# Windowed attention in a conv-attention-expert kernel: the mask product on 64 array rows, the products of a block grouped by array tile, the projection behind the second turn of the probabilities

## The chip, the cores and the metric

The kernel runs on one core of a Trainium2 chip. The time is device microseconds of one execution, given as the median of several. The profile shows one execution, with all engines of the core: TensorE (PE for its matrix products, PEld for its weight loads), VectorE (DVE), ScalarE (ACT), GpSimd (POOL) and the DMA queues.

## The reference, cut to what matters

Eight images of 64 channels and 32x32 pixels go through two deformable convolutions, then through windowed attention and then through a layer of experts. The change touches the attention alone:

```python
q  = (x @ Wq.T).reshape(b, t, h, e) / scale          # t = 1024 tokens, h = 8 heads, e = 64
kk = (xp @ Wk.T).reshape(b, tp, h, e) / scale        # xp: x padded by k-1 tokens ahead
v  = (xp @ Wv.T).reshape(b, tp, h, e)
idx = jnp.arange(t)[:, None] + jnp.arange(k)[None, :]     # k = 32: each token sees 32 keys
dot  = jnp.einsum('bthe,btkhe->bthk', q, kk[:, idx])
attn = jax.nn.softmax(dot, axis=-1)
out  = jnp.einsum('bthk,btkhe->bthe', attn, v[:, idx])
return out.reshape(b, t, h * e) @ Wu.T + bu
```

## The kernel before

The two convolutions come first (span 0 to about 415 us), then a layer norm, the attention (437 to 679 us), a second layer norm and the experts. Heads are folded into two sets of weights ahead of the attention: `a_heads` (queries times keys) and `b_heads` (values times the output projection).

The attention works on 32 blocks: 4 pairs of images, 8 blocks of 128 tokens each. Each block goes through a pipeline that is written out by hand, with one order per engine; a body of four blocks is looped seven times with a register, and an eighth body follows unrolled. Counting semaphores join the engines. On TensorE one block `b` of the loop (`body`, L908) does, in this order:

- `queries` of block b+4 (L821): eight products in fp32, each of 64 rows by 128 columns of the array, into banks 0 and 1 of the result memory. In the trace every fp32 product is two instructions, so a block shows 16.
- `values` of block b, image 0 (L888): eight products on array tiles of 64x64, into banks 5 and 6.
- `turn_probs` of block b+1, image 0 (L869): four transposes on the whole 128x128 array, into bank 4.
- `scores` of block b+3: two mask products in fp16 with 512 columns (L834), each on 32 rows by 128 columns, that start banks 2 and 3 with a large negative number where a key is outside a token's window; then sixteen products on 64x128 (L844) that add the scores.
- `values` of block b, image 1 (L888), then `turn_probs` of block b+1, image 1 (L869).
- `turn_keys` of block b+2 (L857): two transposes on 128x128 into bank 7.
- `project_values` of block b (L903): eight products on 128x64, into bank 7.

The waits of `values` stand in `before_values` (L873). In most blocks they are given as `carry`, so that they are written ahead of the last product of `queries` or of `scores`, and `values` itself starts with no wait.

ScalarE's block (L971) is: copies of the query results (L950), copy of the values of image 0 out of banks 5 and 6 (L968), copy of the turned probabilities of image 0 (L962), copy of the values of image 1, of the turned probabilities of image 1, and the exponentials of block b+3 (L956). VectorE's block (L1035) is: row maxima and their subtraction for block b+3 (L1007, L1009), copy of the turned keys (L1023), the join of the projection to the tokens (L1033), then sums and reciprocals for block b+3 (L1015, L1017). GpSimd scales the probabilities (L1085) and copies the windows of block b+4 onward (L1069, L1077).

Three lines set what `values` waits for. A copy of values raises `z_ready` by one (L968); VectorE raises it by one ahead of the loops (L1045); and `before_values` waits for a count (L878):

```python
    nc.vector.tensor_copy(at.mark[:, 0:1], m.bu[:, 0:1]).then_inc(at.z_ready, 1)      # L1045
                   m.ps[:, 5:7, image * 2 * P:(image + 1) * 2 * P]).then_inc(at.z_ready, 1)   # L969
        pe.wait_ge(at.z_ready, (i * BODY + b) * 2 + image + 1)                        # L878
```

Of the kernel before, what the change touches and what calls it, by code (L numbers as in the profile page):

```python
# [15 lines left out]
NIMG, C, H, W = 8, 64, 32, 32  # L16
PAIRS = NIMG // 2
P = 128
# [655 lines left out]
HG = 2  # L674
# [119 lines left out]

TURN_AHEAD, KEYS_AHEAD, SCORES_AHEAD, QUERIES_AHEAD = 1, 2, 3, 4
ALL_BLOCKS = PAIRS * BLOCKS
BODY = 4
TURNS = ALL_BLOCKS // BODY  # L800
# [4 lines left out]
def exists(i, b):  # L805

    return not isinstance(i, int) or i * BODY + b < ALL_BLOCKS


def attention_pe(nc, pe, m, at):  # L810
    def queries(i, b, carry=None):

        pe.wait_ge(at.windows_ready, i * BODY + b + 1)
        if b:
            pe.wait_ge(at.g_ready, (i * BODY + b) * 2)
        for h in range(H4):
            for image in range(2):
                rows = slice(C * image, C * image + C)
                if carry is not None and (h, image) == (H4 - 1, 1):
                    carry()  # L820
                last = nc.tensor.matmul(m.ps[:, image, h * P:(h + 1) * P], at.a_heads[rows, h, :],  # L821
                                        at.window[rows, b % 4, WINDOW:SPAN], start=True, stop=True)
                if h == H4 - 1:
                    last.then_inc(at.g_in_psum, 1)

    def scores(i, b, carry=None):

        pe.wait_ge(at.g_ready, (i * BODY + b) * 2 + 2)
        pe.wait_ge(at.swapped_ready, (i * BODY + b) * 2 + 2)
        if b:  # L830
            pe.wait_ge(at.shifted, i * BODY + b)
        for hg in range(HG):
            rows = slice(TQ * hg, TQ * hg + TQ)
            nc.tensor.matmul(m.ps[:, 2 + hg, :], m.spread_q[rows, :], m.mask[rows, :], start=True, stop=False,  # L834
                             skip_group_check=True)
        for image in range(2):
            for j in range(TILES):
                first = (image * TILES + j % 2 * 2 + j // 2) * KEYS
                for hg in range(HG):
                    rows = slice(C * hg, C * hg + C)  # L840
                    keys = at.window if image == hg else at.swapped
                    if carry is not None and (image, j, hg) == (1, TILES - 1, HG - 1):
                        carry()
                    last = nc.tensor.matmul(m.ps[:, 2 + hg, first:first + KEYS], at.g[rows, b % 2, image, j, :],  # L844
                                            keys[rows, b % 4, j * TQ:j * TQ + KEYS], start=False, stop=True,
                                            skip_group_check=True)
        last.then_inc(at.scores_in_psum, 1)

    def turn_keys(i, b):

        if b:
            pe.wait_ge(at.xw_ready, i * BODY + b)
        pe.wait_ge(at.windows_ready, i * BODY + b + 1)
        if b >= KEYS_AHEAD:
            pe.wait_ge(at.added, i * BODY + b)
        for odd in range(2):
            last = nc.tensor.transpose(m.ps[:, 7, (2 + odd) * P:(3 + odd) * P],  # L857
                                       at.window[:, b % 4, odd * TQ:odd * TQ + P], m.identity[:, :])
        last.then_inc(at.xw_in_psum, 1)

    def turn_probs(i, b, image):
        if image == 0:
            pe.wait_ge(at.probs_ready, i * BODY + b + 1)
        if b or image:
            pe.wait_ge(at.pt_ready, (i * BODY + b) * 2 + image)
        for odd in range(2):
            for hg in range(HG):
                k = odd * HG + hg
                last = nc.tensor.transpose(m.ps[:, 4, k * P:(k + 1) * P], at.p[:, b % SLOTS_P, hg, image, odd, :],  # L869
                                           m.identity[:, :])  # L870
        last.then_inc(at.pt_in_psum, 1)

    def before_values(i, b, image):  # L873

        pe.wait_ge(at.pt_ready, (i * BODY + b) * 2 + image + 1)
        if image == 0:
            pe.wait_ge(at.xw_ready, i * BODY + b + 1)
        pe.wait_ge(at.z_ready, (i * BODY + b) * 2 + image + 1)  # L878

    def values(b, image):  # L880

        for odd in range(2):
            first = (image * 2 + odd) * P
            for hg in range(HG):
                k = odd * HG + hg
                for late in range(2):
                    rows = slice(KEYS * late, KEYS * late + KEYS)
                    last = nc.tensor.matmul(m.ps[C * hg:C * hg + C, 5 + late, first:first + P],  # L888
                                            at.xw[rows, b % 2, odd, C * image:C * image + C],
                                            at.pt[rows, image, k * P:(k + 1) * P], start=True, stop=True,  # L890
                                            skip_group_check=True)
        last.then_inc(at.z_in_psum, 1)

    def project_values(i, b):
        pe.wait_ge(at.z_ready, (i * BODY + b) * 2 + 3)
        if not exists(i, b + KEYS_AHEAD):

            pe.wait_ge(at.added, i * BODY + b + 2)
            pe.wait_ge(at.xw_ready, ALL_BLOCKS)
        z = at.z[:, :, :].rearrange("p a (j h q) -> p a h j q", j=TILES, h=H4)  # L900
        for h in range(H4):
            for image in range(2):
                last = nc.tensor.matmul(m.ps[C * image:C * image + C, 7, 0:P],  # L903
                                        at.b_heads[:, h, :], z[:, image, h, :, :], start=(h == 0), stop=(h == H4 - 1),
                                        skip_group_check=True)
        last.then_inc(at.projected, 1)

    def body(i):  # L908
        for b in range(BODY):
            if exists(i, b + QUERIES_AHEAD):  # L910
                queries(i, b + QUERIES_AHEAD, lambda: before_values(i, b, 0))
            else:
                before_values(i, b, 0)
            values(b, 0)
            if exists(i, b + TURN_AHEAD):
                turn_probs(i, b + TURN_AHEAD, 0)
            if exists(i, b + SCORES_AHEAD):
                scores(i, b + SCORES_AHEAD, lambda: before_values(i, b, 1))
            else:
                before_values(i, b, 1)  # L920
            values(b, 1)
            if exists(i, b + TURN_AHEAD):
                turn_probs(i, b + TURN_AHEAD, 1)
            if exists(i, b + KEYS_AHEAD):
                turn_keys(i, b + KEYS_AHEAD)
            project_values(i, b)

    queries(0, 0)
    turn_keys(0, 0)
    queries(0, 1)  # L930
    scores(0, 0)
    turn_keys(0, 1)
    queries(0, 2)
    scores(0, 1)
    queries(0, 3)
    scores(0, 2)
    for image in range(2):
        turn_probs(0, 0, image)
    with pe.Fori(0, TURNS - 1) as i:
        body(i)  # L940
    body(TURNS - 1)


def attention_act(nc, act, m, at):
# [19 lines left out]
    def values(i, b, image):  # L964
        if image == 0:
            act.wait_ge(at.projected, i * BODY + b + 1)
        act.wait_ge(at.z_in_psum, (i * BODY + b) * 2 + image + 1)
        nc.scalar.copy(at.z[:, image, :].rearrange("p (a n) -> p a n", a=2),  # L968
                       m.ps[:, 5:7, image * 2 * P:(image + 1) * 2 * P]).then_inc(at.z_ready, 1)  # L969

    def body(i):  # L971
        for b in range(BODY):
            if exists(i, b + QUERIES_AHEAD):
                queries(i, b + QUERIES_AHEAD)
            values(i, b, 0)
            if exists(i, b + TURN_AHEAD):
                probs(i, b + TURN_AHEAD, 0)
            values(i, b, 1)
            if exists(i, b + TURN_AHEAD):
                probs(i, b + TURN_AHEAD, 1)  # L980
            if exists(i, b + SCORES_AHEAD):
                exponentials(i, b + SCORES_AHEAD)

    queries(0, 0)
    queries(0, 1)
# [1 line left out]
    exponentials(0, 0)  # L987
    queries(0, 3)
    exponentials(0, 1)
    exponentials(0, 2)  # L990
    for image in range(2):
        probs(0, 0, image)
    with act.Fori(0, TURNS - 1) as i:
# [292 lines left out]
def program(nc, a, out):  # L1286
    ctx = ExitStack()
    with ctx:
# [3 lines left out]
        def sem(name):  # L1292
            return ctx.enter_context(nc.semaphore(name))
# [173 lines left out]
        at.z_ready = sem("at_z_ready")  # L1467
        at.projected = sem("at_projected")
        at.added = sem("at_added")
        at.windows_ready = sem("at_windows_ready")  # L1470
        at.swapped_ready = sem("at_swapped_ready")
        at.exp_ready = sem("at_exp_ready")
# [308 lines left out]
def constants():  # L1781
# [17 lines left out]
    places = places.reshape(4, 2, TAPS, HALVES, HALF_PIX).swapaxes(2, 3).copy()  # L1799
    c["places"] = (places.reshape(4, 2, TAPS * PIX).view(np.uint32) >> 16).astype(np.uint16)  # L1800
    c["identity"] = np.eye(P, dtype=f32)
    c["spread_q"] = np.tile(np.eye(TQ) * MASK_SCALE, (P // TQ, P // TQ)).astype(f16)

    qq, kk = (np.arange(P) % TQ)[:, None], np.arange(KEYS)[None, :]
    c["mask"] = np.tile(np.where((kk > qq) & (kk <= qq + WINDOW), 0.0, MASKED), (1, TILES * HG)).astype(f16)
# [59 lines left out]
```

## Time and profile before

| | us |
|---|---|
| median of 3 runs | 744.38 (742.71 to 757.19) |
| the profiled execution | 749.22 |
| its span | 747.4 |
| mean granted TensorE clock in it | 0.870 of full speed |

Busy time is the sum over an engine's instructions where they don't overlap. Products on TensorE are pipelined and their ends are modelled, so the starts of groups are the safer reading: the time from one group's start to the next group's start is what a group takes of TensorE. In a row of the timeline the first number is the start and the second the length, both in us; "x16" is the number of instructions merged, and the bracket at the end gives the idle time of the engine before the row and what ended it.

### The profile page before, as it was taken

What the parts mean: (1) busy time and instruction counts of PE and PEld (TensorE: products, weight loads), DVE (VectorE), ACT (ScalarE), POOL (GpSimd) and SP (SyncE); (2) the same over time, 40 slices, a digit from 0 to 9 for tenths busy, and PEclk for the clock granted to TensorE, in tenths of its full rate; (3) what the DMA queues carried; (4) which work ended last, traced back from release to release, by engine and by line L of the source; (5) the groups of instructions that cost most, each with busy time, mean ns of one, the idle gap of its engine ahead of it and who ended that gap; (6) DMA issues with size and microseconds to landing.
All of it is one profiled execution on the core that took longest, in us unless ns stands there. A gap on an engine that the chain in (4) does not pass through costs nothing.

```text
span 747.4 us, 32556 instructions
## 1 busy us (share of the span) xinstructions
PE 637.9 (85%) x14954; PEld 474.3 (63%) x14954; DVE 462.7 (62%) x559; ACT 366.7 (49%) x564; POOL 293.1 (39%) x287
## 2 busy tenths in 40 slices
PE   6579888889895899899889487999999999995575
PEld 1146666667651577666668466888888888874353
DVE  0587877675615977777862715576666666665623
ACT  0265566454423655646642324565565565554430
POOL 4045556463510654554551232434434444430400
PEclk9856999896998588979988755999999999998768
DMA  8310000000004000000000720000000000000002
GB/s 300 81 29 3 5 4 5 4 4 4 5 4 89 10 4 4 4 4 5 5 4 4 163 94 1 3 1 0 0 0 0 0 0 0 0 1 1 1 2 117
DMA packets 6403, 18.01 MB, mean 24 GB/s; under 512 B 1869, under 2 KB 4237, under 8 KB 5573
## 3 DMA queue, kind: packets, MB, share of 16 engines
q1 hardware_dynamic: 6286, 16.24, 7.9%
q8 instruction: 99, 1.62, 0.9%
q14 instruction: 18, 0.15, 0.1%
HBM read 12.37 MB, written 3.87 MB: 22 GB/s over the span
## 4 chain that ended last, share of the span: by engine, by line
PE 77%; DVE 6%; ACT 5%; DMA 4%; issue 4%; POOL 1%; SPq 1%; DVEq 0%; ACTq 0%
PE banks L268 21%; PE banks L199 11%; PE banks L844 9%; PE banks L821 5%; PE banks L888 5%; PE banks L869 5%; PE banks L903 4%; PE banks L171 3%; PE banks L185 2%; DMA off<-in_places_dram 2%; ACT y L301 2%; PE banks L834 1%; DMA off<-offsets_dram 1%; PE banks L229 1%; PE banks L615 1%
## 5 line engine op out<-in xcount | busy, mean ns | idle before, releaser
L322 POOL TENSOR_TENSOR y<-hy,hx 128x576 f32<-128x576 f32 (+1 forms) x104 | 167.4, 1631 | 201.1 <-DVE hy L396 191.8
L268 PE MATMUL banks<-y,xt 32*64 32x144 f32 (+1 forms) x6656 | 168.9, 309 | 23.3 <-issue 12.0
L268 PEld LDWEIGHTS banks<-y,xt 32*64 32x64 f32 x6656 | 115.6, 147 | 54.3 <-issue 35.4
L322 DVE TENSOR_TENSOR y<-hy,hx 128x576 f32<-128x576 f32 (+1 forms) x104 | 121.8, 1215 | 5.0 <-DVE hy L396 0.5
L1085 POOL TENSOR_TENSOR y<-y,stats 128x1024 f32<-128x1024 f32 x32 | 60.8, 1900 | 109.2 <-DVE stats L1017 109.2
L349 ACT ACTIVATE hx<-banks 128x768 f32<-128x768 f32 x96 | 62.0, 650 | 60.7 <-PE banks L171 59.7
L354 ACT ACTIVATE hy<-banks 128x768 f32<-128x768 f32 (+1 forms) x92 | 71.7, 805 | 38.8 <-PE banks L185 38.4
L301 DVE COPY y<-banks 128x768 f32<-128x768 f32 x48 | 45.8, 954 | 70.7 <-PE banks L268 70.7
L199 PE MATMUL banks<-y,w_dc 64*64 64x128 f32 x2304 | 85.8, 302 | 3.3 <-issue 2.0
L199 PEld LDWEIGHTS banks<-y,w_dc 64*64 64x64 f32 x2304 | 76.1, 152 | 10.7 <-issue 8.7
L1007 DVE TENSOR_REDUCE stats<-banks 128x16 f32<-128x1024 f32 x32 | 39.2, 1225 | 69.4 <-PE banks L844 69.4
L844 PEld LDWEIGHTS banks<-src,y 64*128 64x128 f32 x1024 | 64.5, 201 | 7.9 <-issue 7.9
L844 PE MATMUL banks<-src,y 64*128 64x64 f32 x1024 | 69.1, 289 | 0.0
L968 ACT COPY hy<-banks 128x512 f32<-128x512 f32 x64 | 38.0, 593 | 62.5 <-PE banks L888 62.5
L396 DVE TENSOR_SCALAR hy<-hy 128x1632 f32<-128x1632 f32 (+2 forms) x48 | 45.7, 953 | 10.3 <-ACT hy L354 10.2
L956 ACT ACTIVATE y<-y 128x1024 f32<-128x1024 f32 x32 | 33.8, 1057 | 27.1 <-DVE y L1009 27.1
L1015 DVE TENSOR_REDUCE stats<-y 128x16 f32<-128x1024 f32 x32 | 38.9, 1217 | 12.9 <-ACT y L956 12.9
L869 PE MATMUL banks<-identity,y 128*128 128x128 f32 x256 | 42.9, 291 | 3.1 <-ACT hy L962 3.1
L301 ACT COPY y<-banks 128x768 f32<-128x768 f32 x48 | 38.1, 794 | 14.3 <-PE banks L268 14.3
L888 PE MATMUL banks<-hy 64*64 64x128 f32 x1024 | 42.7, 282 | 1.7 <-ACT hy L968 1.7
L393 DVE TENSOR_SCALAR hx<-hx 128x1152 f32<-128x1152 f32 x48 | 38.9, 810 | 8.2 <-ACT hx L349 8.2
L821 PE MATMUL banks<-src,s 64*128 64x128 f32 x512 | 41.7, 308 | 1.7 <-ACT src L745 1.1
(140 smaller groups left out, 811.4 us busy)
## 6 DMA issues: line engine op xcount, KB each, us to landing
src<-in_x_dram SPq DMA_DIRECT2D x4, 578.0 KB, 5.7
y<-in_w_dram SPq DMA_DIRECT2D x1, 2080.0 KB
xt<-in_xt_dram SPq DMA_DIRECT2D x1, 2048.0 KB, 11.2
off<-in_w_dram SPq DMA_DIRECT2D x2, 1024.0 KB
out_dram<-tokens SPq DMA_DIRECT2D x4, 512.0 KB, 3.8
offsets_dram<-tokens SPq DMA_DIRECT2D x32, 54.0 KB
off<-offsets_dram SPq DMA_DIRECT2D x16, 108.0 KB
w_dc<-in_w_dc_dram SPq DMA_DIRECT2D x2, 288.0 KB, 9.4
```

Source lines behind the costliest of these rows:

```text
L199: last = nc.tensor.matmul(m.ps[C * g:C * g + C, bank + p // 2, 0:PLACES], cv.w_dc[rows, tap, :], m.sampled[rows, row % 2, p, tap, :], star ...
L268: last = nc.tensor.matmul(ap(out, [[UNIT_ROWS * PITCH - 2, 3], [PITCH, strip.n], [1, WIN_COLS]]), m.xt[32 * j:32 * j + 32, strip.tile_row, ...
L301: return copy(ap(m.sampled[:, unit.row % 2, j, 3 * unit.ky, :], [[TAPS * PLACES, 2], [W, 3 * UNIT_ROWS], [1, W]]), ap(m.ps[:, j, 4:], [[BA ...
L322: multiply(dst, hy, hx, ALU.mult).then_inc(cv.s_ready[g], 1)
L349: nc.scalar.activation(m.hx[:, u % 2, :, first:end], m.ps[:, bank:bank + 2, 0:end - first], ACT.Abs).then_inc(cv.emptied, 1)
L354: nc.scalar.activation(ap(m.hy[:, u % 2, 0, strips[0].at * HAT_ROW:], [[Y_HATS, 2], [HAT_PITCH, 3 * n_rows], [1, W]]), ap(m.ps[:, bank, :] ...
L396: nc.vector.tensor_scalar(hat, hat, 1.0, 1.0, ALU.min, ALU.subtract).then_inc(cv.hats, 1)
L821: last = nc.tensor.matmul(m.ps[:, image, h * P:(h + 1) * P], at.a_heads[rows, h, :], at.window[rows, b % 4, WINDOW:SPAN], start=True, stop ...
L844: last = nc.tensor.matmul(m.ps[:, 2 + hg, first:first + KEYS], at.g[rows, b % 2, image, j, :], keys[rows, b % 4, j * TQ:j * TQ + KEYS], st ...
L869: last = nc.tensor.transpose(m.ps[:, 4, k * P:(k + 1) * P], at.p[:, b % SLOTS_P, hg, image, odd, :], m.identity[:, :])
L888: last = nc.tensor.matmul(m.ps[C * hg:C * hg + C, 5 + late, first:first + P], at.xw[rows, b % 2, odd, C * image:C * image + C], at.pt[rows ...
L1085: nc.gpsimd.tensor_tensor(p, p, scale.unsqueeze(2).to_broadcast([P, 2 * TILES * HG, KEYS]), ALU.mult).then_inc(at.probs_ready, 1)
```

## The change

Five things change, all in the attention.

- `spread_q` is laid out in blocks of 64 rows (32 of the scaled identity, 32 of zeros), and the two mask products use rows 0 to 63 and 64 to 127, as the score products do.
- TensorE's order in a block is: `values` of both images, `turn_probs` of image 0, `queries`, `scores`, `turn_probs` of image 1, `turn_keys`, `project_values`. The `carry` arguments are gone.
- `before_values` ends with a semaphore instruction, `sem_inc` on a new semaphore `values_begun` that nobody waits for, and stands directly ahead of each `values`.
- ScalarE's order in a block is: both copies of values, the exponentials, the turned probabilities of image 0, the query copies, the turned probabilities of image 1.
- The exponentials run for block b+2 instead of b+3 (`EXPS_AHEAD`), so the one of block 2 leaves the part ahead of the loop. VectorE's and GpSimd's code is as before.

```diff
-TURN_AHEAD, KEYS_AHEAD, SCORES_AHEAD, QUERIES_AHEAD = 1, 2, 3, 4
+TURN_AHEAD, KEYS_AHEAD, EXPS_AHEAD, SCORES_AHEAD, QUERIES_AHEAD = 1, 2, 2, 3, 4
...
         for hg in range(HG):
-            rows = slice(TQ * hg, TQ * hg + TQ)
+            rows = slice(C * hg, C * hg + C)
             nc.tensor.matmul(m.ps[:, 2 + hg, :], m.spread_q[rows, :], m.mask[rows, :], start=True, stop=False,
                              skip_group_check=True)
...
         pe.wait_ge(at.z_ready, (i * BODY + b) * 2 + image + 1)
+        pe.sem_inc(at.values_begun, 1)
...
         for b in range(BODY):
-            if exists(i, b + QUERIES_AHEAD):
-                queries(i, b + QUERIES_AHEAD, lambda: before_values(i, b, 0))
-            else:
-                before_values(i, b, 0)
-            values(b, 0)
+            for image in range(2):
+                before_values(i, b, image)
+                values(b, image)
             if exists(i, b + TURN_AHEAD):
                 turn_probs(i, b + TURN_AHEAD, 0)
+            if exists(i, b + QUERIES_AHEAD):
+                queries(i, b + QUERIES_AHEAD)
             if exists(i, b + SCORES_AHEAD):
-                scores(i, b + SCORES_AHEAD, lambda: before_values(i, b, 1))
-            else:
-                before_values(i, b, 1)
-            values(b, 1)
+                scores(i, b + SCORES_AHEAD)
...
         for b in range(BODY):
+            for image in range(2):
+                values(i, b, image)
+            if exists(i, b + EXPS_AHEAD):
+                exponentials(i, b + EXPS_AHEAD)
+            if exists(i, b + TURN_AHEAD):
+                probs(i, b + TURN_AHEAD, 0)
             if exists(i, b + QUERIES_AHEAD):
                 queries(i, b + QUERIES_AHEAD)
-            values(i, b, 0)
-            if exists(i, b + TURN_AHEAD):
-                probs(i, b + TURN_AHEAD, 0)
-            values(i, b, 1)
             if exists(i, b + TURN_AHEAD):
                 probs(i, b + TURN_AHEAD, 1)
-            if exists(i, b + SCORES_AHEAD):
-                exponentials(i, b + SCORES_AHEAD)
...
     exponentials(0, 1)
-    exponentials(0, 2)
...
-    c["spread_q"] = np.tile(np.eye(TQ) * MASK_SCALE, (P // TQ, P // TQ)).astype(f16)
+    spread = np.concatenate([np.eye(TQ) * MASK_SCALE, np.zeros((C - TQ, TQ))])
+    c["spread_q"] = np.tile(spread, (P // C, P // TQ)).astype(f16)
```

## Rows read from the trace of the kernel before

**Rows 1.** Page, part 4: the chain of work that ended last, by engine, then line.

```profile
PE 77%; DVE 6%; ACT 5%; DMA 4%; issue 4%; POOL 1%; SPq 1%; DVEq 0%; ACTq 0%
```

**Rows 2.** Busy time by stretch: stretch, length, five engines (instructions), granted clock, DMA.

```profile
443.00:460.00 17.00, 16.09 (x134) 14.12 (x132) 6.60 (x7) 6.17 (x9) 2.16 (x2) 0.50 0.00 1
480.00:640.00 160.00, 160.00 (x2491) 130.90 (x2487) 105.69 (x139) 96.35 (x162) 65.57 (x93) 1.00 0.00 0
660.00:680.00 20.00, 16.90 (x274) 12.86 (x272) 9.73 (x17) 10.73 (x18) 3.80 (x2) 1.00 0.01 2
```

**Rows 3.** Timeline of TensorE's products, one block of the loop and the next start.

```profile
487.56 1.16 PE L821 MATMUL banks<-src,s 64*128 64x128 f32 x16
488.65 0.67 PE L888 MATMUL banks<-hy 64*64 64x128 f32 x16
489.25 0.66 PE L869 MATMUL banks<-identity,y 128*128 128x128 f32 x4
489.84 0.39 PE L834 MATMUL banks<-mask,spread_q 32*128 32x512 f16 x2
490.15 2.00 PE L844 MATMUL banks<-src,y 64*128 64x64 f32 x32
492.08 0.67 PE L888 MATMUL banks<-hy 64*64 64x128 f32 x16
492.68 0.66 PE L869 MATMUL banks<-identity,y 128*128 128x128 f32 x4
493.17 0.38 PE L857 MATMUL banks<-identity,src 128*128 128x128 f32 x2
493.49 1.09 PE L903 MATMUL banks<-hy,y 128*64 128x128 f32 x16
494.51 0.38 PE L821 MATMUL banks<-src,s 64*128 64x128 f32 x2
```

**Rows 4.** Timeline of all engines, the last block (31).

```profile
675.47 0.67 PE L888 MATMUL banks<-hy 64*64 64x128 f32 x16
...
676.26 0.59 ACT L968 COPY hy<-banks 128x512 f32<-128x512 f32 x1 [1.25 <-PE banks L888]
676.96 0.46 PEld L888 LDWEIGHTS banks<-hy 64*64 64x64 f32 x16 [1.06 <-issue]
676.99 0.67 PE L888 MATMUL banks<-hy 64*64 64x128 f32 x16 [0.85 <-ACT hy L968]
677.71 0.58 ACT L968 COPY hy<-banks 128x512 f32<-128x512 f32 x1 [0.87 <-PE banks L888]
678.35 0.85 PEld L903 LDWEIGHTS banks<-hy,y 128*64 128x64 f32 x16 [0.94 <-ACT hy L968]
```

**Rows 5.** Timeline of the other engines, in and behind the block of rows 3.

```profile
487.77 1.06 ACT L956 ACTIVATE y<-y 128x1024 f32<-128x1024 f32 x1 [0.76 <-DVE y L1009]
...
488.86 1.22 DVE L1015 TENSOR_REDUCE stats<-y 128x16 f32<-128x1024 f32 x1 [0.43 <-ACT y L956]
...
490.51 1.90 POOL L1085 TENSOR_TENSOR y<-y,stats 128x1024 f32<-128x1024 f32 x1 [2.77 <-DVE stats L1017]
...
492.20 1.22 DVE L1007 TENSOR_REDUCE stats<-banks 128x16 f32<-128x1024 f32 x1 [1.84 <-PE banks L844]
```

**Rows 6.** Timeline of all engines, ahead of the loop and in its first block.

```profile
460.52 1.11 PE L869 MATMUL banks<-identity,y 128*128 128x128 f32 x4
...
463.15 1.06 ACT L956 ACTIVATE y<-y 128x1024 f32<-128x1024 f32 x1 [5.53 <-DVE y L1009]
464.12 0.57 ACT L962 COPY hy<-banks 128x512 f32<-128x512 f32 x1
...
464.68 1.90 POOL L1085 TENSOR_TENSOR y<-y,stats 128x1024 f32<-128x1024 f32 x1 [3.98 <-DVE stats L1017]
...
464.74 1.12 PE L869 MATMUL banks<-identity,y 128*128 128x128 f32 x4 [3.10 <-ACT hy L962]
...
474.74 0.67 PE L888 MATMUL banks<-hy 64*64 64x128 f32 x16
```

More of the change, by code:

```diff
@@ L810, in attention_pe, with queries @@
 def attention_pe(nc, pe, m, at):
-    def queries(i, b, carry=None):
+    def queries(i, b):
         pe.wait_ge(at.windows_ready, i * BODY + b + 1)
@@ L818, in queries @@
                 rows = slice(C * image, C * image + C)
-                if carry is not None and (h, image) == (H4 - 1, 1):
-                    carry()
                 last = nc.tensor.matmul(m.ps[:, image, h * P:(h + 1) * P], at.a_heads[rows, h, :],
@@ L824, in queries, with scores @@
                     last.then_inc(at.g_in_psum, 1)
-    def scores(i, b, carry=None):
+    def scores(i, b):
         pe.wait_ge(at.g_ready, (i * BODY + b) * 2 + 2)
@@ L841, in scores @@
                     keys = at.window if image == hg else at.swapped
-                    if carry is not None and (image, j, hg) == (1, TILES - 1, HG - 1):
-                        carry()
                     last = nc.tensor.matmul(m.ps[:, 2 + hg, first:first + KEYS], at.g[rows, b % 2, image, j, :],
@@ L1469, in program @@
         at.added = sem("at_added")
+        at.values_begun = sem("at_values_begun")
         at.windows_ready = sem("at_windows_ready")
```

## The prediction

> **What bounds the kernel now.** I read the page's chain of work first: TensorE stands on 77% of it [rows 1], so time is to be looked for there. Then the busy time by stretch: between 480 and 640 us TensorE is busy for 160.00 of 160.00 us at a granted clock of 1.00, the full 2.4 GHz, while VectorE has 105.69, ScalarE 96.35 and GpSimd 65.57 [rows 2]. So in the loop TensorE alone sets the time, and the other three are hidden as long as none of them makes it wait. Then the timeline of one block. From one `queries` to the next it takes 494.51 - 487.56 = 6.95 us, and the starts of the groups divide it [rows 3]: queries 1.09, values of image 0 0.60, turn 0.59, mask 0.31, scores 1.93, values of image 1 0.60, second turn with keys and projection 1.83 (492.68 to 494.51). All 27 full blocks look alike.
>
> The reader is to see one more thing there. The second turn is followed by the turned keys, which use the same 128x128 tile, and takes 0.49 us (492.68 to 493.17); the first turn is the same four products, is followed by the mask on another tile, and takes 0.59 [rows 3]. So a change of array tile costs about 0.10 us. A block before has eight of them.
>
> **The change part by part.** *Fewer changes of tile.* In the new order they are: values to turn, turn to queries, scores to turn, keys to projection, projection to values; five instead of eight. Two of the three that go are queries to mask and mask to scores, because the mask now has the scores' tile; the third lies between the two groups of values. Queries then take 1.09 - 0.10 = 0.99, the mask 0.31 - 0.10 = 0.21. The mask's count, columns and type stay, so nothing else in it changes. No row shows fp16 products between fp32 ones on one tile: if the change of type empties the array as the change of tile did, these 0.20 us stay. If entering a group costs as well, the gain is larger. I bound the gain by 0 and 0.30 per block for both, the upper end being three times the 0.10 of rows 3, and take 0.20, because the rows show a price for the tile and none for the type.
>
> *The values of both images in a row.* This is what decides. `before_values` for image 1 waits for `z_ready` of 2b + 2. One of these counts comes from the mark ahead of the loop, 2b from the copies of earlier blocks; the last one can only be this block's copy of image 0. So image 1 may not start before ScalarE has copied image 0 out of banks 5 and 6, and that copy waits for image 0's products. Before, `turn_probs` and `scores` stood between the two, 492.08 - 488.65 = 3.43 us of work [rows 3], and covered this round trip. The new order puts nothing between. What it costs uncovered, the trace shows once, in the last block, where nothing is left to put there [rows 4]: image 0 starts at 675.47, the copy runs from 676.26 for 0.59 us, the weights of image 1 follow at 676.96 and its products at 676.99. Start to start that is 1.52 us, with TensorE idle for 0.85 of it. I take 1.52 for every block; ScalarE is free for the copy, as shown below, so the same steps follow each other.
>
> The Trainium skill ("PSUM — Partial Sum Buffer", Terms) says that TensorE writing and ScalarE reading one bank and quadrant at the same time is an error; no run here shows such an overlap, and by this rule the wait can't simply be dropped.
>
> *The semaphore instruction.* No row shows one that raises a count on TensorE. The two per block sit where waits sit already. In rows 4 the way from the copy's end (676.85) to the weight load (676.96), with a wait passed on it, is 0.11 us and is in the 1.52. So the bounds are nothing and another 0.11 per block; I take nothing, as nobody waits for this semaphore and the products ahead are queued already.
>
> *The new block*, from values of image 0: image 1 at 1.52, first turn at 2.12 (+0.60), queries at 2.71 (+0.59), mask at 3.70 (+0.99), scores at 3.91 (+0.21), second turn at 5.84 (+1.93), next block at 7.67 (+1.83). That is 0.72 longer than 6.95.
>
> *Is something else late next?* ScalarE copies image 0 at 0.79 to 1.38 and image 1 (0.72 after its products, rows 4) at 2.24 to 2.83; the exponentials follow, 1.06 [rows 5], to 3.89; then the turned probabilities, 0.57 [rows 6], to 4.5, which the second turn needs at 5.84. The query copies wait behind these two and are needed one block later. The last copy of turned probabilities can't start before the second turn and is done by about 7.1; image 1 of the next block needs it at 9.19. The exponentials run a block later, and VectorE's sums wait in order for them, with the next row maxima queued behind: sums start at 3.95, and from them to GpSimd's start is 490.51 - 488.86 = 1.65 [rows 5], so VectorE is free at about 5.5; the scores of that block end and release the maxima at 3.91 + 2.05 = 5.96 (490.15 to 492.20, rows 3 and 5). Cover 0.5 us. GpSimd ends at 5.6 + 1.90 = 7.5, and the turn that needs it stands at 7.67 + 2.12. So the moved exponentials cost nothing in the loop. No DMA is moved, and GpSimd's queue keeps its order.
>
> *Ahead of the loop.* The second turn of block 0 waited until 464.74 for a copy that stood behind the exponentials of block 2 (463.15) [rows 6]; without them it runs straight behind the first turn of 460.52. But the first turn of block 1 needs GpSimd's product, done at 464.68 + 1.90 = 466.58, and queries and scores now stand behind it. At full clock the next values follow 0.59 + 0.99 + 0.21 + 1.93 + 1.83 = 5.55 later, at 472.2; if the clock stays at half, as it was granted up to 460 [rows 2], up to some 3 us later. I take 474.0 against 474.74: -0.7.
>
> *The end.* From 474.74 to the last projection at 678.35 are 203.61 us [rows 4, 6]. New: 27 blocks of 7.67 are 207.09. Block 28 has no queries: 7.67 - 0.99 = 6.68. Block 29 has no queries and no scores; its second turn waits for the copy behind the exponentials, 3.89 + 0.57 + 0.05 = 4.52, and the block ends 1.83 later, at 6.35. Block 30: image 1's copy to 2.83, turned probabilities to 3.42, second turn at 3.47, then 0.59 and 1.02 (493.49 to 494.51): 5.08. Block 31 is the one of rows 4: 2.88. The sum is 228.08, so +24.47; with -0.7 it is **+23.8 us**.
>
> The profiled execution took 749.22, which gives 773.0. It lies 4.8 above the median shown, and the attention is alike in all of them as far as one trace can tell, so I predict on the median: 744.38 + 23.8 = **768**.
>
> **The rivals.** *Not slower: the second values start on the heels of the first.* Then a block is 6.95 - 0.30 = 6.65 and the kernel gains 27 x 0.30 = 8 us, and about 1 at the ends: 735. It decides as soon as image 1 starts less than 0.80 after image 0 (1.52 - 0.72). For it: the price of a change of tile in rows 3 is plain. Against it: it needs image 0's copy to be no condition, and the count and rows 4 say it is one. The Trainium skill ("TensorEngine Tiling (Array Packing)", Key Properties) states that changing the tiling mode drains TensorE; the 0.59 against 0.49 agree, and by that rule alone the change could only gain.
>
> *The stall is partly covered*, for instance because the copy starts earlier in a dense block than in the last one. Each 0.3 us per block takes 27 x 0.3 = 8 off: 755 to 759.
>
> *Dearer groups*: the fp16 mask still empties the array (0.20 x 28 = 5.6), or the semaphore instruction is on the path (0.11 x 31 = 3.4): 772 to 777.
>
> *The clock falls.* TensorE has a hole of 0.85 us in each block where it had none, and before the loop it was busy for 16.09 of 17.00 us and still granted 0.50, half of 2.4 GHz [rows 2]. At half clock the products take nearly twice as long; if a fifth of the attention ran so, about 40 us of it, some 25 more: 793. Against it: from 660 to 680, with 3.1 us of holes in 20, the grant stayed 1.00 [rows 2].
>
> **How the numbers follow.** Forecast 0.65 (its own range 764 to 772); dearer groups 0.15; clock 0.05; stall partly covered 0.10; on the heels 0.05. The range leaves out the clock case, the second values on the heels and a little of the rest: 756 to 780. The runs before spread from 742.71 to 757.19, so about 2% (15 us) is what can be told from no change. Slower by over 2%, above 759.3: 0.65 + 0.15 + 0.05 = 0.85. Within 2%: the partly covered stall and some of the last case, 0.12. Faster by over 2%, below 729.5: 0.03, should its price of a tile be double.
>
> **What would show it.** In the loop's timeline: image 1 of the values 1.5 us behind image 0, its idle time put down to L968's copy; about 0.99 from queries to mask and 0.21 from mask to scores; a block of 7.67 at a clock of 1.00; TensorE idle for 0.85 us in each block, and VectorE's maxima still released by the scores. I am wrong if image 1 follows within 0.8 us, if TensorE waits for VectorE or GpSimd, or if the clock drops in the loop.

## The result and the profile after

The changed kernel takes 762.25 us (median of 4 runs, 757.20 to 765.58) against 748.39 for the kernel before on the same chips (4 runs, 742.71 to 757.19): a ratio of 1.019 with a 95% interval from 1.013 to 1.026, so it is slower by 10 to 19 us. The range of the prediction holds it. Its centre, 768, was 6 us too high, and its +23.8 us was 10 too much; that only 6 of these 10 show is luck, since the median before, 744.38 when the forecast was made, is 748.39 with a fourth run. The result lies below the 764 to 772 of the forecast's own case. The prediction gave 0.85 to slower by over 2% and 0.12 to within 2%; the measured 1.9% stands at the bound between the two, with an interval on both sides of it. The profiled execution took 760.81 us, with a span of 758.9.

The chain of work, from the page of the changed kernel, now has 7% in which TensorE waited for nothing that the profile shows ("issue"), where it had 4% [rows 1]:

```profile
PE 74%; issue 7%; DVE 6%; ACT 5%; DMA 4%; POOL 2%; SPq 1%; DVEq 0%; POOLq 0%
```

Busy time by stretch in the changed kernel (columns as in rows 2): three stretches ahead of the loop, then the loop.

```profile
441.00:448.50 7.50, 6.87 (x56) 6.19 (x57) 0.42 (x1) 2.15 (x4) 1.12 (x4) 0.50 0.01 4
449.00:458.00 9.00, 6.08 (x96) 5.49 (x96) 6.48 (x7) 5.55 (x7) 0.00 (x0) 1.00 0.01 2
459.00:468.00 9.00, 6.46 (x54) 4.59 (x54) 4.12 (x5) 3.63 (x6) 4.86 (x8) 0.50 0.00 0
480.00:640.00 160.00, 142.53 (x2308) 121.32 (x2304) 96.43 (x129) 88.08 (x148) 59.84 (x88) 1.00 0.00 0
```

In the loop TensorE is busy for 142.53 of 160 us where it had no hole at all [rows 2], still at a granted clock of 1.00. The timeline of one block, all engines, shows where the hole is (the line numbers are the changed kernel's: L885 values, L962 their copy, L865 turns, L819 queries, L832 mask, L840 scores, L853 keys, L900 projection):

```profile
502.85 0.67 PE L885 MATMUL banks<-hy 64*64 64x128 f32 x16
...
503.64 0.59 ACT L962 COPY hy<-banks 128x512 f32<-128x512 f32 x1 [1.34 <-PE banks L885]
...
504.30 0.45 PEld L885 LDWEIGHTS banks<-hy 64*64 64x64 f32 x16 [1.02 <-issue]
504.33 0.67 PE L885 MATMUL banks<-hy 64*64 64x128 f32 x16 [0.81 <-issue]
...
504.93 0.65 PE L865 MATMUL banks<-identity,y 128*128 128x128 f32 x4
...
505.51 1.16 PE L819 MATMUL banks<-src,s 64*128 64x128 f32 x16
...
506.50 0.38 PE L832 MATMUL banks<-mask,spread_q 64*128 64x512 f16 x2
506.51 1.97 PEld L840 LDWEIGHTS banks<-src,y 64*128 64x128 f32 x32
...
506.72 1.90 PE L840 MATMUL banks<-src,y 64*128 64x64 f32 x32
...
508.55 0.66 PE L865 MATMUL banks<-identity,y 128*128 128x128 f32 x4
508.67 1.23 DVE L1000 TENSOR_REDUCE stats<-banks 128x16 f32<-128x1024 f32 x1 [0.53 <-PE banks L840]
...
509.35 1.09 PE L900 MATMUL banks<-hy,y 128*64 128x128 f32 x16
...
510.38 0.67 PE L885 MATMUL banks<-hy 64*64 64x128 f32 x16
```

Image 1 of the values starts 504.33 - 502.85 = 1.48 us behind image 0. The copy of image 0 lies between them, from 503.64 to 504.23. It is the pattern of rows 4, now in every block. The profile calls the gap "issue". The likely reason, which no run shows by itself, is that the wait sits in the new semaphore instruction and not on the weight load: the last projection of the same kernel, which has no such instruction ahead of it, is put down to the copy (696.18 below). That the copy ends 0.07 us ahead of the weight load tells what it waited for. The block is 510.38 - 502.85 = 7.53 us long, against 6.95 [rows 3]. The projection stands behind the second turn in both kernels, so what the title says of it names no difference.

Four starts cut the attention of each kernel into a head, 27 blocks of the loop and an end: the first queries, the projections of blocks 0 and 27, and the last projection. In the timeline of the changed kernel:

```profile
441.00 2.08 PE L819 MATMUL banks<-src,s 64*128 64x128 f32 x16 [1.10 <-ACT src L745]
...
471.78 1.09 PE L900 MATMUL banks<-hy,y 128*64 128x128 f32 x16
...
674.62 1.09 PE L900 MATMUL banks<-hy,y 128*64 128x128 f32 x16
...
696.18 1.09 PE L900 MATMUL banks<-hy,y 128*64 128x128 f32 x16 [0.69 <-ACT hy L962]
```

and in that of the kernel before, whose last projection is in rows 4:

```profile
437.25 2.08 PE L821 MATMUL banks<-src,s 64*128 64x128 f32 x16 [1.10 <-ACT src L745]
...
472.63 1.09 PE L903 MATMUL banks<-hy,y 128*64 128x128 f32 x16
...
660.37 1.09 PE L903 MATMUL banks<-hy,y 128*64 128x128 f32 x16
```

| us | before | after | difference | forecast |
|---|---|---|---|---|
| head | 35.38 | 30.78 | -4.6 | +0.4 |
| 27 blocks | 187.74 | 202.84 | +15.1 | +19.4 |
| end | 17.98 | 21.56 | +3.6 | +4.0 |
| sum | 241.10 | 255.18 | **+14.1** | **+23.8** |

The forecast column is the prediction's own sum, cut at the same starts (its 474.0 for the values of block 1 is 472.98 for the projection ahead of them, 1.02 earlier). The +14.1 us of the attention agree with the +13.9 of the medians. Outside the attention the same code differs from one execution to the next, since the granted clock falls in other places: behind the last projection are 69.1 us in one profile and 62.7 in the other, at a mean clock of 0.78 and 0.84. Profiled again, the kernel before took 62.2 us there and the changed one 69.5, so this difference is not the change's.

### The profile page after: what moved, and what is told of

It reads as the page before. It is cut to its first block, busy times and chain, and to the rows that moved or that the text cites. A ratio compares the mean times of both kernels' runs of the same rounds, so it can differ in the third digit from the quotient of the medians.

```text
span 758.9 us, 32581 instructions
## 1 busy us (share of the span) xinstructions
PE 624.1 (82%) x14954; PEld 471.1 (62%) x14954; DVE 460.7 (61%) x559; ACT 366.5 (48%) x564; POOL 291.4 (38%) x287
## 4 chain that ended last, share of the span: by engine, by line
PE 74%; issue 7%; DVE 6%; ACT 5%; DMA 4%; POOL 2%; SPq 1%; DVEq 0%; POOLq 0%
PE banks L268 21%; PE banks L199 11%; PE banks L840 7%; PE banks L885 5%; PE banks L865 5%; PE banks L819 5%; PE banks L900 4%; PE banks L171 3%; PE banks L185 2%; DMA off<-in_places_dram 2%; ACT y L301 2%; DMA off<-offsets_dram 1%; PE banks L229 1%; PE banks L615 1%; PE banks L832 1%
## 5 line engine op out<-in xcount | busy, mean ns | idle before, releaser
L268 PE MATMUL banks<-y,xt 32*64 32x144 f32 (+1 forms) x6656 | 169.6, 311 | 23.8 <-issue 13.1
L199 PE MATMUL banks<-y,w_dc 64*64 64x128 f32 x2304 | 87.4, 306 | 4.1 <-issue 3.0
L199 PEld LDWEIGHTS banks<-y,w_dc 64*64 64x64 f32 x2304 | 77.7, 154 | 11.6 <-issue 9.4
L962 ACT COPY hy<-banks 128x512 f32<-128x512 f32 x64 | 37.5, 586 | 67.7 <-PE banks L885 67.7
L885 PE MATMUL banks<-hy 64*64 64x128 f32 x1024 | 43.6, 286 | 25.4 <-issue 24.7
L840 PEld LDWEIGHTS banks<-src,y 64*128 64x128 f32 x1024 | 63.6, 191 | 1.0
L840 PE MATMUL banks<-src,y 64*128 64x64 f32 x1024 | 61.8, 271 | 0.0
L956 ACT COPY hy<-banks 128x512 f32<-128x512 f32 x64 | 37.3, 582 | 41.8 <-PE banks L865 41.8
L885 PEld LDWEIGHTS banks<-hy 64*64 64x64 f32 x1024 | 28.8, 135 | 38.0 <-issue 38.0
L865 PE MATMUL banks<-identity,y 128*128 128x128 f32 x256 | 43.3, 293 | 4.1 <-ACT hy L956 2.9
L301 ACT COPY y<-banks 128x768 f32<-128x768 f32 x48 | 38.1, 795 | 14.9 <-PE banks L268 14.9
```

Of the source, the lines that this page charges most:

```text
L199: last = nc.tensor.matmul(m.ps[C * g:C * g + C, bank + p // 2, 0:PLACES], cv.w_dc[rows, tap, :], m.sampled[rows, row % 2, p, tap, :], star ...
L268: last = nc.tensor.matmul(ap(out, [[UNIT_ROWS * PITCH - 2, 3], [PITCH, strip.n], [1, WIN_COLS]]), m.xt[32 * j:32 * j + 32, strip.tile_row, ...
L301: return copy(ap(m.sampled[:, unit.row % 2, j, 3 * unit.ky, :], [[TAPS * PLACES, 2], [W, 3 * UNIT_ROWS], [1, W]]), ap(m.ps[:, j, 4:], [[BA ...
```

## The experiments

The theory: the round trip from the values of image 0 through ScalarE's copy to image 1 has lost its cover and costs about 1 us per block; three changes of array tile less give back part of it. The rivals: the gap comes from the semaphore instruction or from TensorE itself; and the mask's place between fp32 products, not its tile, is what empties the array.

### The wait taken away: values of image 0 in banks 0 and 1

```diff
 queries:        if b:
                     pe.wait_ge(at.g_ready, (i * BODY + b) * 2)
+                if b >= QUERIES_AHEAD:
+                    pe.wait_ge(at.z_ready, (i * BODY + b - QUERIES_AHEAD) * 2 + 2)
 before_values:      pe.wait_ge(at.xw_ready, i * BODY + b + 1)
+                    ahead = (i * BODY + b + QUERIES_AHEAD) * 2
+                    pe.wait_ge(at.g_ready, min(ahead, 2 * ALL_BLOCKS) if isinstance(i, int) else ahead)
-                pe.wait_ge(at.z_ready, (i * BODY + b) * 2 + image + 1)
+                pe.wait_ge(at.z_ready, (i * BODY + b) * 2 + 1)
 values:         ... m.ps[C * hg:C * hg + C, 5 + late, first:first + P]
+                ... m.ps[C * hg:C * hg + C, 5 * image + late, first:first + P]
 ScalarE's copy: ...
-                       m.ps[:, 5:7, image * 2 * P:(image + 1) * 2 * P]).then_inc(at.z_ready, 1)
+                       m.ps[:, 5 * image:5 * image + 2, image * 2 * P:(image + 1) * 2 * P]).then_inc(at.z_ready, 1)
```

> The changed kernel, with the values of image 0 in banks 0 and 1 instead of 5 and 6, so that the values of image 1 need not wait for the copy of image 0 (the queries wait for that copy instead, and the values of image 0 for the query copies). Theory (the copy's round trip between the two groups of values is the loss): image 1 starts about 0.45 us behind image 0 instead of 1.47, a block takes about 6.5 us instead of 7.52 and 6.95 before, and the kernel takes 727 to 737 us, less than both. Rival (the gap comes from the semaphore instruction or from the array itself, not from the copy): image 1 still starts about 1.5 behind, the block stays near 7.5 and the time near 762.

Measured: 726.68 us against 748.38, a ratio of 0.966 (0.957 to 0.974), a little under the 727 to 737 expected. In its timeline both groups of values run as one, and the turn follows:

```profile
517.77 1.10 PE L889 MATMUL banks<-hy 64*64 64x128 f32 x32
518.56 1.07 ACT L966 COPY hy<-banks 128x512 f32<-128x512 f32 x2 [1.34 <-PE banks L889]
518.81 0.66 PE L867 MATMUL banks<-identity,y 128*128 128x128 f32 x4
...
524.26 0.99 PE L889 MATMUL banks<-hy 64*64 64x128 f32 x28
```

From the first product of the values to the turn are 1.04 us for both images, where the changed kernel takes 504.93 - 502.85 = 2.08. Its block is 524.26 - 517.77 = 6.49 us long; the whole gap of 1.04 per block is gone. The copies are as long as before, and the semaphore instruction is still in it; so neither that instruction nor the array sets the gap, and the wait for the copy does. This is also the version that beats both kernels. Its block is 0.46 us shorter than that of the kernel before, 12.4 us over 27 blocks: 0.31 are the mask's two changes of tile (below), and the 0.15 left fall to the third, between the values, which no run varied by itself. Another 5.0 us are its shorter head, below.

### The gap covered: the turn between the two groups of values

```diff
                 before_values(i, b, image)
                 values(b, image)
-            if exists(i, b + TURN_AHEAD):
-                turn_probs(i, b + TURN_AHEAD, 0)
+                if image == 0 and exists(i, b + TURN_AHEAD):
+                    turn_probs(i, b + TURN_AHEAD, 0)
```

> The changed kernel, with the first turn of probabilities between the two groups of values. Theory: image 1 still starts 1.47 us behind image 0, because the copy takes as long as before, but the turn (0.59) now lies inside that time; a block takes 7.52 - 0.59 = 6.93 us, about as much as the kernel before (6.95), and the time is 743 to 751. Rival (TensorE's own groups set the 1.47): the turn adds to it, image 1 starts 2.0 or more behind, and the block stays at 7.5 or above.

Measured: 749.58 us, the median of ten runs, one of which took 810.42 at a mean granted clock of 0.697; 0.997 of the kernel before (0.992 to 1.002). The timeline of TensorE's products:

```profile
543.55 0.67 PE L885 MATMUL banks<-hy 64*64 64x128 f32 x16
544.15 0.66 PE L865 MATMUL banks<-identity,y 128*128 128x128 f32 x4
545.02 0.67 PE L885 MATMUL banks<-hy 64*64 64x128 f32 x16 [0.22 <-issue]
545.62 1.16 PE L819 MATMUL banks<-src,s 64*128 64x128 f32 x16
...
550.49 0.67 PE L885 MATMUL banks<-hy 64*64 64x128 f32 x16
```

Image 1 starts 1.47 us behind image 0, as without the turn, and the turn lies inside: a block of 6.94. The start of image 1 is fixed by the copy, and what stands between is free up to that point; a hole of 0.22 is left.

### The tile of the mask product alone

On the kernel before:

```diff
-            rows = slice(TQ * hg, TQ * hg + TQ)
+            rows = slice(C * hg, C * hg + C)
```

with the new layout of `spread_q`; and the reverse on the changed kernel.

> The kernel before, with the mask product on 64 rows alone. Theory (a change of array tile costs, a change of type does not): mask to scores 0.21 us instead of 0.31 and scores to the next group 1.83 instead of 1.93, a block of 6.75 us instead of 6.95, and 5 to 6 us less in all, 743 against 748. Rival (the fp16 product empties the array in any case): block 6.95, no change of time.

> The changed kernel, with the mask product back on 32 rows. Theory: queries to mask 1.09 us instead of 0.99, mask to scores 0.31 instead of 0.21, scores to turn 1.93 instead of 1.83, so 7.52 + 0.30 = 7.83 us per block and about 8 us more than the changed kernel in the loop. Rival (type, not tile): 7.52.

Measured: 739.14 us with 64 rows on the kernel before, a ratio of 0.984 (0.977 to 0.991); 775.90 in a single run with 32 rows on the changed kernel. The timeline of the kernel before with 64 rows:

```profile
530.41 0.39 PE L834 MATMUL banks<-mask,spread_q 64*128 64x512 f16 x2
530.64 1.89 PE L844 MATMUL banks<-src,y 64*128 64x64 f32 x32
532.46 0.67 PE L888 MATMUL banks<-hy 64*64 64x128 f32 x16
```

and of the changed kernel with 32:

```profile
545.91 1.16 PE L819 MATMUL banks<-src,s 64*128 64x128 f32 x16
547.00 0.39 PE L832 MATMUL banks<-mask,spread_q 32*128 32x512 f16 x2
547.32 2.00 PE L840 MATMUL banks<-src,y 64*128 64x64 f32 x32
549.25 0.66 PE L865 MATMUL banks<-identity,y 128*128 128x128 f32 x4
```

With 64 rows mask to scores is 0.23 us and scores to the next group 1.82; with 32 they are 0.32 and 1.93, and queries to mask 1.09 instead of the 0.99 of the changed kernel. The mean blocks of the loop are 6.75 and 7.82 us (the second without its first block, part of which ran at half clock), as the theory had it, 0.20 less and 0.31 more than without the edit. The fp16 product between fp32 ones costs nothing that can be seen; its tile did. A change of tile costs 0.10 at the end of the group that it follows, as rows 3 had shown, and about 0.10 more inside the scores that follow it. The weight loads show where this second part lies. In the kernel before, the scores' first load starts only with their first product, at 490.15:

```profile
490.15 1.86 PEld L844 LDWEIGHTS banks<-src,y 64*128 64x128 f32 x32 [0.23 <-issue]
```

In the changed kernel, where mask and scores have one tile, it starts under the mask, at 506.51, 0.21 us ahead of the scores' first product at 506.72.

The gain of mask64, 9.2 us, is more than its loop gives (27 x 0.20 = 5.4); the rest is in the head, below.

### The exponentials put back to the end of ScalarE's block

```diff
-            if exists(i, b + EXPS_AHEAD):
-                exponentials(i, b + EXPS_AHEAD)
...
+            if exists(i, b + SCORES_AHEAD):
+                exponentials(i, b + SCORES_AHEAD)      # behind probs(..., 1)
...
+    exponentials(0, 2)                                 # ahead of the loop
```

> The changed kernel, with the exponentials back at the end of ScalarE's block, for block b+3 (and the one of block 2 ahead of the loop). Theory (the exponentials had to move, because at the end of the block they wait for VectorE and hold up the copy of the next block's image 0): the exponentials run at about 0.9 to 2.0 us of the next block, the copy follows only then, image 1 starts 2.7 us behind image 0 instead of 1.47, a block takes about 8.7 us and the kernel some 790. Rival (ScalarE has room in any order, the copy is not held up): 7.52 per block, 762.

Measured: 823.23 us in a single run. The timeline, products and ScalarE:

```profile
558.16 0.67 PE L885 MATMUL banks<-hy 64*64 64x128 f32 x16
558.97 1.06 ACT L950 ACTIVATE y<-y 128x1024 f32<-128x1024 f32 x1 [1.35 <-DVE y L1003]
559.93 0.57 ACT L962 COPY hy<-banks 128x512 f32<-128x512 f32 x1
560.57 0.45 PEld L885 LDWEIGHTS banks<-hy 64*64 64x64 f32 x16 [1.98 <-issue]
560.60 0.67 PE L885 MATMUL banks<-hy 64*64 64x128 f32 x16 [1.77 <-issue]
```

and busy time by stretch:

```profile
500.00:600.00 100.00, 81.49 (x1194) 69.51 (x1192) 49.71 (x67) 48.14 (x78) 31.50 (x45) 0.91 0.00 0
600.00:700.00 100.00, 83.33 (x1048) 71.29 (x1044) 44.01 (x60) 42.49 (x69) 28.28 (x40) 0.80 0.00 0
530.00:603.00 73.00, 57.11 (x920) 48.54 (x918) 39.64 (x53) 37.04 (x60) 23.81 (x35) 1.00 0.00 0
```

The copy stands behind the exponentials, which wait for VectorE; image 1 starts 2.44 us behind image 0. The mechanism is the expected one, the place a little earlier (2.7 was expected). At full clock its blocks take 8.49, and 27 x (8.49 - 7.51) = 26 us more than the changed kernel would be some 790, not 823. Most of the rest is the clock: the grant no longer stays at 1.00 in the loop, and its mean block is 9.57, another 27 x 1.08 = 29. Why it fell stays open. It fell again and again in blocks with holes of 1.77 us, but from 530 to 603 us it stayed at 1.00 with the same holes; this is a single execution, and the kernel with the turn between the values, whose profile has holes of 0.22, also had one at a mean clock of 0.697. So the moved exponentials were a needed part of the change, and the rival of the falling clock, which the changed kernel doesn't show, appeared in this run.

### One change of tile less on top

The kernel with the values of image 0 in banks 0 and 1, and both turns behind the scores. ScalarE copies both behind the query copies, and the second turn, now in bank 5, waits for the copy of the values of image 1 out of that bank:

```diff
-            if exists(i, b + TURN_AHEAD):
-                turn_probs(i, b + TURN_AHEAD, 0)       # behind values
...
+            for image in range(2):                      # behind scores; image 1 in bank 5
+                if exists(i, b + TURN_AHEAD):
+                    turn_probs(i, b + TURN_AHEAD, image)
```

> The kernel with the values of image 0 in banks 0 and 1, and one change of tile less: both turns of probabilities stand together behind the scores, the second in bank 5 instead of 4, and ScalarE copies them behind the query copies. Theory (a change of tile costs what the entry and the exit showed, 0.15 to 0.20 us, and no wait takes its place): a block of 6.30 to 6.35 us instead of 6.49, some 4 us less in the loop, 719 to 727. Rival (the turned probabilities now come too late for the next block's values, or VectorE's sums hold up the row maxima, 0.2 us by the times of the rows): TensorE idle ahead of the values, a block of 6.5 or more, no gain.

Measured: 734.21 us, 0.975 of the kernel before (0.966 to 0.984), not below the 726.68. The timeline of its values, their copies and the queries:

```profile
530.32 1.10 PE L891 MATMUL banks<-hy 64*64 64x128 f32 x32
...
531.11 1.07 ACT L967 COPY hy<-banks 128x512 f32<-128x512 f32 x2 [1.29 <-PE banks L891]
531.81 1.00 PEld L821 LDWEIGHTS banks<-src,s 64*128 64x128 f32 x16 [0.63 <-issue]
531.84 1.16 PE L821 MATMUL banks<-src,s 64*128 64x128 f32 x16 [0.42 <-ACT hy L967]
```

The theory missed. The block of 6.5 or more and the missing gain of its rival came, but by another wait than the rival named. The queries write the banks that the values of image 0 now use, so they wait for that copy, and the turn that was moved away had covered this wait. TensorE is idle for 0.42 us, and the block is 6.82 instead of 6.49. It is the mistake of the change itself, made once more in another place.

### The head: three kernels profiled again

No edit: the kernel before, the changed one, and the kernel before with the mask on 64 rows.

> The kernel before again, for the clock ahead of the loop. In the first profile it was granted 0.50 from the first queries to the loop. Theory (the 64-row mask product raises the clock early): 0.50 again until the loop is reached, about 37 us from the first queries to the values of block 1. Rival (which clock is granted there changes from run to run): some stretch at 1.00, a shorter head.

> The changed kernel again, for the clock ahead of the loop. Theory (the 64-row mask product raises the clock early): again 1.00 from about 8 us after the first queries for some 10 us, and about 32 us from the first queries to the values of block 1. Rival (chance): as in the kernel with the turn between the values, 0.50 until the loop, 37 us or more.

> The kernel before with the mask product on 64 rows, again, for the clock ahead of the loop. Theory (the 64-row mask product raises the clock early): a stretch at 1.00 between the first queries and the loop, and a head some 4 us shorter than in the kernel before. Rival (chance): 0.50 until the loop.

The three came as the theory had them. The head goes from the first queries to the projection of block 0; the last column is the clock granted from the first queries to the first products of the loop:

| kernel | mask rows | head, us | granted ahead of the loop |
|---|---|---|---|
| before, twice | 32 | 35.4, 35.8 | 0.50 throughout |
| changed, mask on 32 rows | 32 | 38.1 | 0.50 throughout |
| changed, twice | 64 | 30.8, 30.6 | 1.00 for 10 us |
| before, mask on 64 rows, twice | 64 | 31.4, 31.1 | 1.00 for 7 and 10 us |
| values in banks 0 and 1 | 64 | 30.4 | 1.00 for 7 us |
| the same, both turns behind the scores | 64 | 29.9 | 1.00 for 7 us |
| turn between the values | 64 | 37.7 | 0.50 throughout |

A stretch of the repeated kernel before, then one of the mask on 64 rows, repeated:

```profile
440.00:450.00 10.00, 9.37 (x74) 7.70 (x70) 2.61 (x3) 2.15 (x4) 0.00 (x0) 0.50 0.00 0
```

```profile
440.00:450.00 10.00, 7.08 (x112) 6.49 (x112) 6.61 (x7) 5.55 (x7) 0.06 (x1) 0.99 0.01 2
```

The kernel before and the same with the mask on 64 rows differ in the mask alone, and their heads lie 4.0 and 4.7 us apart; that is the part of mask64's gain that its loop doesn't give. The changed kernel and the same with the mask on 32 rows lie 7.3 apart. None of three profiles with 32 rows had the full clock ahead of the loop, seven of eight with 64 rows had it (the kernel with the exponentials at the end too, not in the table). The exception, with the turn between the values, does the same work ahead of the loop as the changed kernel. So the wider mask goes with an earlier full clock, but it doesn't settle it by itself; what else does stays open. That the mask is the cause is argued from these pairs and not shown; no run varied the head's work further.

## Why the prediction was right, and where its sizes were off

**The step that decides was right.** `z_ready` counts this block's copy of image 0, the work that covered it had gone, and the price was the one of rows 4: 1.52 forecast, 1.48 measured. Moving image 0 to other banks removed exactly this.

**The term of the loop** came out at 0.56 us per block (202.84 - 187.74 over 27) instead of 0.72. Two terms are behind most of it. The scores took 508.55 - 506.72 = 1.83 instead of 1.93, because a change of tile costs on entry as well; the prediction had named this and priced it at nothing. The stall was 0.04 shorter. The other starts agree within 0.02 each. 27 x 0.16 = 4.3 us.

**The head** was the larger miss for its size: -4.6 instead of +0.4. The prediction had the clock at half as far as the loop or, at worst, longer, and saw no way for it to rise earlier than before. In the changed kernel it was at 1.00 from 449 to 458, and queries, mask and scores ran there at full speed. These 5.0 us, the 4.3 of the loop and 0.4 of the end are the 9.7 by which the sum was too high.

**The end** agrees: the second turn of block 29 waits for the copy behind the exponentials, and the four last steps take 21.56 us against 22.0 forecast.

**What cost nothing** did so: the row maxima were released by the scores after 0.53 us of idle time on VectorE (0.5 forecast), GpSimd was never waited for in the loop, and the semaphore instruction leaves the two groups of values of the first experiment running as one. It was not taken out by itself. The sign on the profile was forecast wrongly in one point: the idle time is not put down to the copy but to "issue".

**The rivals.** "On the heels" did not happen in the changed kernel; the first experiment is that case made real, and its block of 6.49 is 0.16 better than the 6.65 worked out for it, because the price of a tile was set too low. "Partly covered" came to 0.04 us per block of the 0.3 that it was worked out for. "Dearer groups" fell with the two mask kernels and the first experiment. The clock stayed at 1.00 in the loop. The Trainium skill ("TensorEngine Tiling (Array Packing)", Key Properties) says that a change of tiling mode drains TensorE; the traces agree, with 0.10 us before and about 0.10 behind such a change.

## What to carry to other kernels

Work that stands between a product and a second product into the same banks is cover for the copy between them; before grouping products by tile, look for the wait that the work in between was hiding, and read its uncovered price where a loop runs out. Where the order is worth having, move one of the results to banks that are free at that time, and look at once who waits for those. A regular loop forecasts well from starts of groups; a stretch in which the granted clock can change does not.

## What the runs showed of the hardware

- A change of array tile costs about 0.20 us where an fp16 mask product stands ahead of fp32 scores: 0.32 to 0.23 from mask to scores, 1.93 to 1.82 for the scores. The change of type alone showed no price.
- TensorE was busy for 25.05 of the 29.70 us from 437.30 to 467.00 in the kernel before and was granted 0.50, 1.2 GHz, all that time; in the changed kernel it rose to 1.00, 2.4 GHz, 7.5 us after the first queries, with 6.87 of 7.50 us busy before. What decides between the two stays open.
- Holes of 0.81 us in each block of 7.5 left the clock at 1.00. With holes of 1.77 in each block of some 8.5 it stayed at 1.00 from 530 to 603 us and fell again and again around that stretch (0.91 and 0.80 over 100 us each), in one execution.
- On a change of tile the weight load of the scores started only with their first product (490.15); on one tile it started 0.21 us ahead of it, under the mask (506.51 and 506.72).
